# A four-layer graph network on one core: layer ends merged tile by tile with the next layer's first projection piece

## The reference

```python
x = _layernorm(x + L0(x))        # L0: norm, two GAT layers, then [x, out2] @ Wu + bu
x = _layernorm(x + L1(x))        # L1: two relational GAT layers over 3 edge types

# L1, a layer:
xr = einsum('nd,rdf->rnf', x, W)                  # the projection, 3 relations
alpha = leaky_relu(xr[etype, dst] @ q + xr[etype, src] @ k, 0.2)
e = exp(alpha - segment_max(alpha, dst)[dst])
out = segment_sum(e / (z[dst] + EPS) * xr[etype, src], dst) + b
# between the two layers of L1: h = elu(h)
```

## Time and profile before

| | us |
|---|---|
| three runs | 2136.81, 2138.81, 2141.84 (median 2138.81) |
| the profiled execution, as timed | 2136.87 |
| its span in the profile | 2135.0 |
| PE busy | 1907.5 (89%) |
| DVE busy | 1310.0 (61%) |
| ACT busy | 705.8 (33%) |
| mean granted PE clock | 0.954 |

### The profile page before, as it was taken

One profiled execution on the slowest core, in us unless ns is written; L12 is line 12 of the kernel. 1 busy time (PEld: TensorE's weight loads), 2 busy tenths in 40 slices (PEclk: granted clock), 3 DMA queues, 4 the chain that ended last, 5 costly groups with the idle time before them and its releaser, 6 DMA issues. The chain is left out here.

```text
span 2135.0 us, 23258 instructions
## 1 busy us (share of the span) xinstructions
PE 1907.5 (89%) x7980; PEld 1306.0 (61%) x7981; DVE 1310.0 (61%) x2104; ACT 705.8 (33%) x1138; POOL 19.5 (1%) x38
## 2 busy tenths in 40 slices
PE   5789978599796769999699979997999989999997
PEld 3445534499552335555599979996555545555554
DVE  7769858699506660999699979994260022252253
ACT  5768945444013311111244434443111111131131
POOL 0000001000000000000000000000000000000000
PEclk9989989799998889999899989999999999999999
DMA  5100069341332232553221122112462133223243
GB/s 152 73 8 28 28 221 306 117 138 31 108 95 75 83 128 98 195 192 118 96 82 55 55 73 81 58 52 74 136 212 96 60 125 131 84 84 128 83 131 132
DMA packets 112564, 225.48 MB, mean 106 GB/s; under 512 B 11743, under 2 KB 68950, under 8 KB 109498
## 3 DMA queue, kind: packets, MB, share of 16 engines
q1 hardware_dynamic: 81706, 169.65, 24.5%
q10 hardware_dynamic: 27472, 40.12, 5.5%
q0 software_dynamic: 3264, 14.16, 2.4%
HBM read 171.12 MB, written 52.76 MB: 105 GB/s over the span
## 5 line engine op out<-in xcount | busy, mean ns | idle before, releaser
L998 PE MATMUL ps<-work 128*128 128x193 f32 (+1 forms) x3200 | 532.8, 330 | 45.1 <-DVE work L1589 45.1
L998 PEld LDWEIGHTS ps<-work 128*128 128x128 f32 x3200 | 531.9, 192 | 46.2 <-issue 46.2
L1583 DVE SCALAR_TENSOR_TENSOR work<-work,sd 128x1280 f32<-128x1280 f32 (+2 forms) x270 | 337.5, 1251 | 350.2 <-PE ps L1015 240.5
L1266 ACT ACTIVATE work<-work,s 128x1280 f32<-128x1280 f32 (+2 forms) x270 | 303.0, 1125 | 624.4 <-DVE work L1583 624.2
L970 PE MATMUL ps<-work 128*128 128x384 f32 (+2 forms) x1440 | 468.5, 488 | 1.8 <-ACT work L1211 1.8
L1015 PE MATMUL ps<-work 128*128 128x385 f32 (+1 forms) x1200 | 392.5, 489 | 13.3 <-DVE work L1589 9.5
L970 PEld LDWEIGHTS ps<-work 128*128 128x128 f32 x1440 | 273.1, 190 | 194.9 <-issue 18.3
L1015 PEld LDWEIGHTS ps<-work 128*128 128x128 f32 x1200 | 228.8, 191 | 177.0 <-issue 18.4
L1589 DVE SCALAR_TENSOR_TENSOR work<-work,counts 128x1280 f32<-128x1280 f32 (+2 forms) x270 | 320.9, 1188 | 8.3 <-ACT work L1266 8.0
L1251 ACT ACTIVATE work<-ps 128x384 f32<-128x384 f32 x120 | 59.0, 492 | 335.5 <-PE ps L970 328.1
L1419 DVE TENSOR_SCALAR work<-work,winoff 125x480 bf16<-125x480 f16 x480 | 157.7, 397 | 0.1
(11 more groups left out here) (188 smaller groups left out, 1059.6 us busy)
## 6 DMA issues: line engine op xcount, KB each, us to landing
work<-hx_d SPq DMA_DIRECT2D x90, 384.0 KB, 3.0
work<-pqrow_d SPq DMA_DIRECT2D x18, 1280.0 KB, 6.5
hx_d<-work ACTq DMA_DIRECT2D x120, 192.0 KB, 1.9
work<-nomask_d SPq DMA_DIRECT2D x70, 320.0 KB, 3.4
nomask_d<-work SPq DMA_DIRECT2D x40, 320.0 KB, 6.7
work<-hx_d SPq DMA_DIRECT2D x120, 96.0 KB, 1.9
feat<-srow_d SPq DMA_DIRECT2D x3, 2560.0 KB, 12.4
work<-in_wt_c POOLq DMA_DIRECT2D x6, 1152.0 KB, 11.2
```

What stands on the lines that cost most here:

```text
L998: last = mm(sums_at(c, t, u), xe[i % RING][:, t * P:(t + 1) * P], hx[:, i % RING, 0:1 + c.width], start=(r == 0 and k == 0 and t % TB == 0 ...
L1266: nc.scalar.activation(xe[i % RING][:, 0:n_], xe[i % RING][:, 0:n_], ACT.Exp, bias=s02[:, k, bass.ds(rh, 1)], scale=0.8).then_inc(s.exp_do ...
L1583: v.scalar_tensor_tensor(xe[i % RING][:, 0:n_], pqb[slot][:, 0, lo:lo + n_], sd[:, k, bass.ds(rh, 1)], pqb[slot][:, 1, lo:lo + n_], ALU.ad ...
```

## The change

Phase 4 is gone as a phase. PE's and ACT's programs of the third layer now take a tile's steps one after the other. PE: `second_layer(0)`, `second_layer(1)`, `turn(0)`, then for each t `second_layer(t + 2)`, `project(t)`, `turn(t + 1)`. The second layer's product has one set of four banks (4 to 7), the turned tile has banks 2 and 3, the first piece's sums have banks 0 and 1. ACT: the square root of tile t + 1, then the copy of projection t with its store, then the copy of turned tile t + 1. DVE has `first_norm` ahead of the scan.

Seven tiles of `base_d` are loaded during layer b's attention, straight to their place in `feat`; tiles 3, 4 and 5, whose place is still in use then, at the start of the third layer. `o2T` is in two pieces, of which the second lies in `wring[1]`; so `w_load(1)` is issued by ACT after the last turned tile's copy. The three first mask loads stand behind the stores of x1 in SP's queue.

In the last layer PE has `turn(0)`, `turn(1)`, then for each t `project(t)`, `turn(t + 2)`; ACT takes the exponential of tile t + 2, the copy of turned tile t and the copy of projection t - 1. In the third layer the rows `pq` are turned ahead of the last projection instead of behind it (the last number of `Conv`, 0 to 1).

```diff
-C = Conv("c", [0, 1, 2], 4, 192, 384, 8, 2, 2, True, 0)
+C = Conv("c", [0, 1, 2], 4, 192, 384, 8, 2, 2, True, 1)
...
-        o2T = carve(work, (RING + 4) * NP + 2 * 769, 2 * NP).rearrange("p (h n) -> p h n", h=2)
+        o2T = [carve(work, (RING + 4) * NP + 2 * 769, NP), carve(work, XT_END + DT * 408, NP)]
...
+        BASE_FIRST = [t for t in range(T) if (t + 1) * D <= 2560 or t * D >= 2560 + T * H2C]
+        BASE_LAST = [t for t in range(T) if t not in BASE_FIRST]
...
+                if c is C:
+                    for t in BASE_LAST:
+                        base_load(t, y_x2)
+                    for t in range(T):
+                        sp.wait_ge(y_done, t + 1)
+                        sp.dma_start(x1_d[t * P:(t + 1) * P, :], featv[:, t, :]).then_inc(y_out, 16)
...
+                    for t in BASE_FIRST:
+                        base_load(t, y_x)
...
-            for t in range(8):
-                x_load(t)
-            for t in range(T):
-                sp.wait_ge(y_done, t + 1)
-                if t < T - 8:
-                    x_load(t + 8)
-                sp.dma_start(x1_d[t * P:(t + 1) * P, :], featv[:, t, :]).then_inc(y_out, 16)
-            sp.wait_ge(y_out, 16 * T)
-            end_phase(sp, 4)
...
+                def turn(t):
+
+                    pe.wait_ge(y_done if c is C else elu_done, t + 1)
+                    places = 1 if c is C else 2
+                    if t >= places:
+                        pe.wait_ge(*s.xt_done.at(t - places + 1))
+                    for j in range(DT):
+                        at = (2 + t % places * 2) * 512 + j * P
+                        last = nc.tensor.transpose(ps[:, at:at + P], featv[:, t, j * P:(j + 1) * P], identf[:, :])
+                    last.then_inc(s.turned.sem, 1)
+
+                def second_layer(t):
+
+                    if t:
+                        pe.wait_ge(y_mm_used, t)
+                    for h in range(2):
+                        for q in range(2):
+                            last = mm(bank(4 + h * 2 + q, 384 + q), o2T[h][0:K2, t * P:(t + 1) * P],
+                                      wub[0:K2, h, q * 384:(q + 1) * 384 + q], start=True, stop=True)
+                    last.then_inc(y_mm, 1)
...
+                    if i == 0:
+                        pe.wait_ge(*s.xt_done.at(t + 1))
+                        if n >= 2:
+                            pe.wait_ge(*s.proj_ev.at(n - 1))
+                    else:
+                        pe.wait_ge(*s.proj_ev.at(n - 3))
...
+                if c is C:
+                    second_layer(0)
+                    second_layer(1)
+                    turn(0)
+                    for t in range(T):
+                        if t + 2 < T:
+                            second_layer(t + 2)
+                        project(t)
+                        if t + 1 < T:
+                            turn(t + 1)
+                if c is DD:
+                    turn(0)
+                    turn(1)
+                    for t in range(T):
+                        project(t)
+                        if t + 2 < T:
+                            turn(t + 2)
...
+                if c is C:
+
+                    w_load(0)
+                    y_deviation(0)
+                    fetch_turned(0)
+                    for t in range(T):
+                        if t + 1 < T:
+                            y_deviation(t + 1)
+                        fetch_projected(t)
+                        if t + 1 < T:
+                            fetch_turned(t + 1)
+                        if t == T - 2:
+                            act.wait_ge(y_mm, T)
+                            w_load(1)
+                if c is DD:
+                    w_load(0)
+                    w_load(1)
+                    elu_exp(0)
+                    elu_exp(1)
+                    for t in range(T):
+                        if t + 2 < T:
+                            elu_exp(t + 2)
+                        fetch_turned(t)
+                        if t:
+                            fetch_projected(t - 1)
+                    fetch_projected(T - 1)
...
+                        if n == c.s_rows_at:
+                            if c is C:
+                                act.wait_ge(y_out, 16 * T)
+                            copy_rows(srow_t, ci, c.RH, srow_c)
...
-            for t in range(T):
-                act.wait_ge(y_std, t + 1)
-                nc.scalar.activation(sdev[:, 0, t:t + 1], mv[:, t, 1:2], ACT.Sqrt, bias=epsc[:, 0:1]).then_inc(y_sqrt, 1)
-            end_phase(act, 4)
```

220 lines of the change are left out of this document (97 added, 123 removed).

## The result

The changed kernel ran in 2101.91 us (median of 4 runs, 2100.06 to 2110.19), the kernel before in 2137.81 us (4 runs, 2135.57 to 2141.84). The ratio is 0.9838, 95% interval 0.9807 to 0.9868. The profiled execution has a span of 2099.5 us for 2135.0 before, 35.5 us less. Several terms of the sum failed. The largest are the end of the merged stage, priced at 8.4 us and measured at 5.39, and the clock's loss of 2.0 us at its start, which was not paid there.

A forecast was written before the change was run, and what follows sets the result against it. Before the change, DVE, then a stop without PE work and transposes, then PE bound the third layer's start. Gains of 26.2 (there), 0.6 (score rows) and 0.7 (last layer) sum to 27.5 us: 2138.81 becomes 2111.3, range 2105 to 2119.

The forecast's parts named there:

- the end of the merged stage: Third layer's start, from project(9) to project(10): projection, 3.3 us waiting for the second piece's weights, 1.0 for the clock; 8.4 us.
- the clock's loss of 2.0 us at its start: Start of the third layer's merged stage, before project(0): one PE clock restart, 4 us at half clock, costing 2.0 us.

## What to carry to other kernels

A duration read from a group that stands alone holds its drain; for work that will stand in a row, take the distance between two starts, and if the trace has none, keep the difference for the range. Before a wait in a loop is called thin, follow the delay a second time round: if it meets a longer wait of its own engine, it ends there. At the ends of such a merged loop the overlapping work runs out, and the waits that it hid come out: order the last rounds, and the loads behind them, for themselves. A change can also move the clock's falls in work that it doesn't touch, so compare such stretches over several kernels before they are called noise.

## What the runs showed of the hardware

- A table load that carries no wait of its own ran 1.28 us right behind the barrier (721.69), beside the other engines; with a wait for the tile's statistics it came after them (728.01 in the run with the late load) and DVE waited 1.70 us for 0.36. In the built programs it carried none where one wait stood between DMA and root, and one where two stood there.
- A DMA queued on ACT behind a copy went out 0.02 us after the copy's start, and ran beside it (799.10, 799.12); in the run with one more copy 0.05 us after it (799.79, 799.84).
- The granted clock after short stops: still 1.00 after 1.31, 1.30 and 1.01 us in the changed kernel, fallen to 0.50 after one of 2.32 us in the run with one more copy. After the same two stops at the barrier, 1.36 and 2.63 us, it fell in one execution within SL(1), in another at its start, in a third only after turn(0). A single profile therefore fixes the start of this stage to no better than 3 us.
- In the last layer's attention the same stop of 1.93 us stands twice in the kernel before and in the changed one, with 155.44 us of unbroken work between the two in both. Behind the second the granted clock fell in all three kernels with the old start of the third layer (0.83 over 10 us in the one before) and in none of the nine listed with the new one (1.00 in the changed kernel).
